# Two routed expert layers: one block for normalisation, gates and routing, a region of rows per expert, weights that are waited for expert by expert

## The reference, cut to what matters

```
def _L1_ffn_ref(inputs, gate_w, w1, w2):        # x = x + this(_layernorm(x))
    logits = tokens @ gate_w                    # (2048, 8)
    probs = softmax(logits); expert_idx = argmax(probs)
    mask1 = one_hot(expert_idx, 8)
    pos = cumsum(mask1, axis=0) - 1.0           # place of a row within its expert
    sec_mask = mask1 * one_hot(pos, 320)        # rows past 320 of an expert get nothing
    h = relu(expert_input @ w1[e])              # w1: (8, 256, 1024)
    out = probs of the expert * (h @ w2[e])     # w2: (8, 1024, 256)
def _L3_ffn_ref(x, gate_w, w1, b1, w2, b2):     # the same without a capacity,
    h = gelu(x_flat @ w1[e] + b1[e])            # with gelu and with biases
    y = h @ w2[e] + b2[e]
```

## Time and profile before

| what | value |
|---|---|
| median of 3 runs | 3418.19 us (3417.17 to 3421.18) |
| profiled execution, its own time | 3417.33 us |
| its span in the trace | 3415.7 us |
| busy: PE, DVE, ACT, POOL | 86%, 61%, 55%, 38% of the span |
| routing of layer 1 (1846.98 to 1902.96) | 55.98 us |
| routing of layer 3 (3151.09 to 3208.98) | 57.89 us |
| experts' tiles of layer 1, of layer 3 | 170.67 us, 171.63 us |

### The profile page before, as it was taken

One profiled execution on the slowest core, in us unless ns is written; L12 is line 12 of the kernel. 1 busy time (PEld: TensorE's weight loads), 2 busy tenths in 40 slices (PEclk: granted clock), 3 DMA queues, 4 the chain that ended last, 5 costly groups with the idle time before them and its releaser, 6 DMA issues. The chain is left out here.

```text
span 3415.7 us, 68343 instructions
## 1 busy us (share of the span) xinstructions
PE 2921.4 (86%) x26674; PEld 2033.7 (60%) x26675; DVE 2085.7 (61%) x3098; ACT 1895.5 (55%) x2864; POOL 1302.8 (38%) x942
## 2 busy tenths in 40 slices
PE   6779998737879998889997695979999999988596
PEld 3246665415446666456666694766666666667595
DVE  6968887587867873877873224855444444466122
ACT  3448886293558884568883111755555555456131
POOL 2259998020258883157782212720000000045212
PEclk8979999878989999989997897979999999999698
DMA  4611111200022220022214311011000000042612
GB/s 147 221 56 57 54 54 57 91 13 13 1 59 53 53 47 15 16 47 58 56 38 149 114 37 45 2 31 50 26 26 26 26 26 1 1 109 62 222 37 69
DMA packets 218052, 193.21 MB, mean 57 GB/s; under 512 B 126837, under 2 KB 176865, under 8 KB 216737
## 3 DMA queue, kind: packets, MB, share of 16 engines
q1 hardware_dynamic: 210247, 172.30, 17.4%
q0 software_dynamic: 5280, 14.42, 1.3%
q10 hardware_dynamic: 2233, 2.39, 0.2%
HBM read 112.72 MB, written 39.00 MB: 44 GB/s over the span
## 5 line engine op out<-in xcount | busy, mean ns | idle before, releaser
L2663 POOL TENSOR_TENSOR lta_p_lo<-lta_p,lta_p_hi 128x1024 f16<-128x1024 f32 x256 | 539.0, 2133 | 218.0 <-DVE lta_p_hi L2786 218.0
L2858 ACT ACTIVATE lta_p<-lta_banks,lw_gmax 128x512 f32<-128x512 f32 x512 | 324.0, 683 | 112.7 <-PE lta_banks L2701 108.4
L2769 DVE TENSOR_REDUCE lta_s_ps<-lta_s_ps 128x1 f32<-128x1101 f32 x240 | 314.1, 1309 | 106.7 <-PE lta_s_ps L2680 106.7
L3814 PE MATMUL m_y_ps<-m_w,m_hT 128*128 128x256 f16 x3072 | 355.8, 273 | 2.4 <-DVE m_hT L3972 2.4
L3802 PE MATMUL m_h_ps<-m_x,m_w 128*128 128x512 f16 x1536 | 353.1, 380 | 3.1 <-issue 3.1
L3972 DVE TENSOR_TENSOR m_hT<-m_h,m_hT 128x512 f16<-128x512 f32 x256 | 176.9, 692 | 277.0 <-ACT m_hT L3899 275.3
L3899 ACT ACTIVATE m_h<-m_h_ps,m_h_bias,m_h_scale 128x512 f32<-128x512 f32 x256 | 199.5, 779 | 261.1 <-PE m_h_ps L3802 253.0
L3814 PEld LDWEIGHTS m_y_ps<-m_w,m_hT 128*128 128x128 f16 x3072 | 299.2, 98 | 65.4 <-issue 8.2
L1242 POOL TENSOR_TENSOR c0a_tri_p_lo<-c0a_tri_p,c0a_tri_p_hi 128x1024 f16<-128x1024 f32 (+2 forms) x192 | 285.7, 1526 | 58.2 <-DVE c0a_tri_p_hi L1416 57.4
L3802 PEld LDWEIGHTS m_h_ps<-m_x,m_w 128*128 128x128 f16 x1536 | 150.5, 98 | 159.5 <-issue 5.4
L1491 ACT ACTIVATE c0a_tri_p<-c0a_banks,c_size 128x512 f32<-128x512 f32 (+3 forms) x384 | 208.4, 577 | 45.4 <-PE c0a_banks L1310 32.6
(11 more groups left out here) (760 smaller groups left out, 6582.4 us busy)
## 6 DMA issues: line engine op xcount, KB each, us to landing
m_w<-in_L_ffn_w_dram SPq DMA_DIRECT2D x4, 8192.0 KB, 40.4
m_raw<-in_L_ffn_W_dram SPq DMA_DIRECT2D x16, 1024.0 KB, 6.4
lta_q<-ltb_qT SPq DMA_DIRECT2D x96, 128.0 KB, 2.5
c_side<-in_fside_Bx16xSxS_dram SPq DMA_DIRECT2D x16, 616.0 KB, 4.7
c0a_tri_q<-c_near SPq DMA_DIRECT2D x96, 96.0 KB
c0a_tri_k<-c_mixed SPq DMA_DIRECT2D x93, 96.0 KB
lta_k<-ltb_kT SPq DMA_DIRECT2D x64, 137.6 KB, 2.6
lt_vh<-ltb_v SPq DMA_DIRECT2D x64, 128.0 KB
```

The source lines that it names most:

```text
L2663: nc.gpsimd.tensor_tensor(p_lo[:, slot, :], p32[:, p32_slot(h, j), :], p_hi[:, slot, :], ALU.subtract).then_inc(rested, 1)
L2769: nc.vector.tensor_reduce(ntop_of(h)[:, n:n + 1], scores(h, n), AX_X, ALU.max, negate=True).then_inc(top_ready, 1)
L2858: nc.scalar.activation(p32[0:rows, slot, c * 512:(c + 1) * 512], t_ps[0:rows, c, :], ACT.Exp, bias=bias, scale=p["gmax"][0:rows, 0:1]).the ...
L3814: last = nc.tensor.matmul(y_ps[:, q, 0:D], hT[:, k % 2, a, f, q * P:(q + 1) * P], w2[:, v, b, f, :], start=f == 0 and m == 0, stop=f == FC ...
```

## The change

1. **One block.** `route_tokens` no longer calls `layernorm_stage`. One block normalises, transposes, gates and routes, in groups of four tiles: `choose(g)`, `place_rows(g)` and `carry(g)` on DVE, `turn`, `gates` and `count(g)` on PE, `keep_rows` and `exponentials(g)` on ACT. The count of earlier groups is carried in `before`. DVE normalises the first eight tiles ahead, and four more after each of the first two groups is placed.
2. **A region per expert.** `sorted_x` grows to `E * T + E * P` = 17,408 rows: expert e owns the rows from e * 2048. A row's address then needs no totals, and POOL scatters group by group (`x_slot`). The compact numbering (`slot`) is kept for `sorted_y`, and a new table `row_of` says where the rows of each of the 23 tiles lie.
3. **Rows loaded by POOL.** The loads of `xs` move from SP to POOL, since their address now comes from `row_of`. For tile j POOL issues the load of tile j + 2 and then waits for `y_evac` of tile j and stores it.
4. **Weights expert by expert.** 16 transfers of 1 MB with a semaphore for each expert. In the experts' block SP waits for an expert's weights, issues a transfer of one number into `flag`, waits for it, and goes on to the next expert; `copy_w` and `reduce` wait for `expert_ready` of their expert.
5. **Zero fills.** The two stores of zeros leave the first stage. Each half of the latent attention fills one `sorted_x` (17.8 MB) with four transfers, issued by ACT after the first exponentials of heads 4, 6, 8 and 10.

```
@@ project_qkv, sync
-        for rows, kept in zip(env.sorted_x, env.zero_stored):
-            sp.dma_start(rows.rearrange("(j p) d -> p j d", p=P),
-                         env.zero[:].unsqueeze(1).to_broadcast([P, NT, D])).then_inc(kept, 16)
@@ latent_attend, scalar
+                if j == 0 and h in ZERO_AT:
+                    act.dma_start(zeros[ZERO_AT.index(h)], env.zero[:].unsqueeze(1).to_broadcast([P, SORTED_ROWS // P // ZERO_FILLS, D])
+                                  ).then_inc(env.zero_stored[b], 16)
@@ route_tokens, sync
-        sp.dma_start(w1[:], w("w1").rearrange("e (c p) f -> p e c f", p=P)).then_inc(weights_loaded, 16)
-        sp.dma_start(w2[:], w("w2").rearrange("e (c p) d -> p e c d", p=P)).then_inc(weights_loaded, 16)
+        for e in range(E):
+            sp.dma_start(w1[:, e], w("w1")[e].rearrange("(c p) f -> p c f", p=P)).then_inc(w_loaded[e], 16)
+            sp.dma_start(w2[:, e], w("w2")[e].rearrange("(c p) d -> p c d", p=P)).then_inc(w_loaded[e], 16)
@@ route_tokens, gpsimd
         for t in range(TILES):
-            nc.gpsimd.indirect_dma_start(sorted_x, bass.IndirectOffsetOnAxis(ap=slot[:, t:t + 1], axis=0),
+            if t % GROUP == 0:
+                pool.wait_ge(slot_ready, t // GROUP + 1)
+            nc.gpsimd.indirect_dma_start(sorted_x, bass.IndirectOffsetOnAxis(ap=x_slot[:, t:t + 1], axis=0),
                                          xn[:, t, :], None).then_inc(scattered, 16)
         pool.wait_ge(scattered, 16 * TILES)
@@ route_tokens, vector
+        for t in range(2 * GROUP):
+            normalise(t)
+        for g in range(groups):
+            choose(g)
+            dve.wait_ge(hot_ready, g + 1)
+            if g:
+                carry(g)
+            place_rows(g)
+            if g == 0:
+                carry(g)
+            if g + 2 < groups:
+                for t in tiles_of(g + 2):
+                    normalise(t)
@@ routed_experts, sync
-        def load(j, u):
-            if not (isinstance(j, int) and j < 2):
-                sp.wait_ge(x_turned, j - 1)
-            sp.dma_start(xs[:, u, :], sorted_x[bass.ds(j * P, P), :]).then_inc(xs_loaded[u], 16)
-        tiles(sp, load)
+        for e in range(E):
+            sp.wait_ge(w_loaded[e], 32)
+            sp.dma_start(flag[0:1, e:e + 1], env.eps[0:1, 0:1]).then_inc(expert_ready, 16)
+            sp.wait_ge(expert_ready, 16 * (e + 1))
@@ routed_experts, gpsimd
-        def store(j, u):
+        def load(j, u):
+            row = pool.value_load(row_of[0:1, bass.ds(j, 1)], min_val=0, max_val=SORTED_ROWS - P)
+            if not (isinstance(j, int) and j < 2):
+                pool.wait_ge(x_turned, j - 1)
+            nc.gpsimd.dma_start(xs[:, u, :], sorted_x[bass.ds(row, P), :]).then_inc(xs_loaded[u], 16)
+
+        def work(j, u):
+            if within(j, 2):
+                load(j + 2, u)
             pool.wait_ge(y_evac, j + 1)
             nc.gpsimd.dma_start(sorted_y[bass.ds(j * P, P), :], ys[:, u, :]).then_inc(ys_stored[u], 16)
 
-        tiles(pool, store)
+        for j in range(2):
+            load(j, j)
+        tiles(pool, work)
@@ routed_experts, tensor, reduce (and vector, copy_w)
             e = pe.value_load(expert_of[0:1, bass.ds(j, 1)], min_val=0, max_val=E - 1)
+            pe.wait_ge(expert_ready, 16 * e + 16)
```

More of the change, by code:

```diff
@@ L3055, in _ @@
     def _(pe):
[L3056 to L3059, removed]
-        nc.tensor.matmul(place_ps[:, 0:TILES * E], upto[:], hot[:].rearrange("p t e -> p (t e)"), start=True, stop=False)
-        for t in range(TILES - 1):
-            later = TILES - 1 - t
-            last = nc.tensor.matmul(place_ps[:, (t + 1) * E:TILES * E].rearrange("p (t e) -> p t e", e=E), all_ones[:],
-                                    hot[:, t:t + 1, :].to_broadcast([P, later, E]), start=False, stop=later == 1)
@@ L3065, in _, with turn, gates @@
-        last.then_inc(counted, 1)
+        def turn(t):
+            pe.wait_ge(normed, t + 1)
+            if t >= TURNED:
+                pe.wait_ge(x_evac, t - TURNED + 1)
+            for c in range(DC):
+                last = nc.tensor.transpose(x_ps[:, t % TURNED, c * P:(c + 1) * P], xn[:, t, c * P:(c + 1) * P], env.ident[:])
+            last.then_inc(x_turned, 1)
+        def gates(t):
+            g, q = divmod(t, GROUP)
+            pe.wait_ge(x_evac, t + 1)
+            if t == 0:
+                pe.wait_ge(gate_loaded, 16)
+            if q == 0 and g >= 2:
+                pe.wait_ge(shifted, g - 1)
+            for c in range(DC):
+                last = nc.tensor.matmul(lg_ps[:, g % 2, q * E:(q + 1) * E], xnT[:, c, t * P:(t + 1) * P], gate[:, c, :],
+                                        start=c == 0, stop=c == DC - 1)
+            if q == GROUP - 1:
+                last.then_inc(lg_done, 1)
@@ L3068, in _, with keep_rows, exponentials @@
             nc.tensor.transpose(b_ps[:, 0:E * FC], b1_rows[:], env.ident[0:E * FC, 0:E * FC]).then_inc(b1_turned, 1)
+        for t in range(TILES + 2):
+            if t >= 2 * GROUP and t % GROUP == 0:
+                count(t // GROUP - 2)
+            if t < TILES:
+                turn(t)
+            if t >= 2:
+                gates(t - 2)
+        count(groups - 1)
+        if b1 is not None:
+            pe.wait_ge(b1_kept, 1)
+        pe.wait_ge(carried, groups)
+        nc.tensor.matmul(b_ps[:, 0:E], all_ones[:], before[:, groups, :], start=True, stop=True).then_inc(summed, 1)
     @block.scalar
     def _(act):
-        act.wait_ge(shifted, 1)
-        nc.scalar.activation(pr[:], lg[:], ACT.Exp).then_inc(exped, 1)
+        def keep_rows(t):
+            act.wait_ge(x_turned, t + 1)
+            nc.scalar.copy(xnT[:, :, t * P:(t + 1) * P],
+                           x_ps[:, t % TURNED, 0:D].rearrange("p (c t) -> p c t", c=DC)).then_inc(x_evac, 1)
+        def exponentials(g):
+            part = slice(g * GROUP, (g + 1) * GROUP)
+            act.wait_ge(shifted, g + 1)
+            nc.scalar.activation(pr[:, part], lg[:, part], ACT.Exp).then_inc(exped, 1)
+        act.wait_ge(var_ready, 1)
+        nc.scalar.activation(rstd[:], var[:], ACT.Sqrt).then_inc(std_ready, 1)
+        nc.scalar.activation(warm[:], env.eps[:], ACT.Exp).then_inc(table_loaded, 1)
+        act.wait_ge(table_loaded, 1)
         if b1 is not None:
@@ L3076, in _ @@
             nc.scalar.copy(b1[:].rearrange("p e c -> p (e c)"), b_ps[:, 0:E * FC]).then_inc(b1_kept, 1)
-            act.wait_ge(b1_kept, 1)
+        for t in range(TILES):
+            keep_rows(t)
+            if t > GROUP and t % GROUP == 2:
+                exponentials(t // GROUP - 1)
+        exponentials(groups - 1)
     @block.vector
```

208 lines of the change are left out of this document (132 added, 76 removed).

## The result

The kernel takes 3544.31 us after the change (median of 4 runs, 3543.13 to 3547.55), against 3417.68 before (median of 4 runs). The ratio is 1.0372, with a 95% interval from 1.0354 to 1.0390: 3.7% slower. The forecast was 3485, with a range that ended at 3540. The direction was right, and about half of the loss had no term in the sum.

A forecast was written before the change was run, and what follows sets the result against it. PE bound the experts' tiles; in routing, the gates-to-scatters chain and the weight transfers ended almost together. 3415.7 + 74 - 6.6 = 3483 of span, 3485.6 with the offsets to the median, gave 3485 us; range 3440 to 3540.

The forecast's parts named there:

- Rows loaded by POOL: Experts' loop: loads behind stores land late, 1.7 us a tile in layer 1, 2.0 in layer 3; 74 us added.
- Zero fills: First stage and latent attention: removed stores and added fills count nothing; upper bound 29 us from ACT's issues.
- forecast as 8 us more: Experts' loop: a 600 ns register load on POOL would make the gap 0.9, not 0.7, adding 8 us.
- the tile's sum: Experts' loop: each of 20 tiles a layer pays the late load of rows, 34 and 40 us, 74 together.
- the 8.5 to 10 that I had named: Experts' loop, a sign to look for: tiles should take 8.5 to 10 us instead of 7.3.
- one tile in five at half speed: Experts' loop, rival: idling PE lowers the granted clock, adding 8 x 7.3 = 58 us, to 3543; chance 3%.
- Routing in groups: Routing: first scatter at 13.2 us, last from 35.4 to 39.3, end near 45, 11 us earlier than 55.98.
- Weights by expert: Start of the experts' block: first product at 55.6 and 58.5 us, gains of 3.8 and 2.8, together 6.6.
- the first rival: Experts' loop: rows arrive in time, tiles keep 7.3 us, routing's gain remains: 3411, at best 3399; chance 11%.
- The flag ahead of the queue: Start of the experts' block, bound: a flag passing SP's queued weights gives 49 and 51, gaining up to 19.
- 1.11 us for every issue: Experts' loop, upper bound: longest issues and gaps make rows 3.0 and 2.5 us late, 116 us in all.
- The sum's own range: Whole kernel: bounds of the terms added, +35 to +116 us, that is 3453 to 3534.

The follow-up runs named there:

- experiment 10: Kernel after, with POOL still waiting for tile j's results, then issuing the load of tile j + 3 ahead of tile j's store: 3509.95 us, ratio 1.0268.
- experiment 1: Kernel before, with only the loads of rows moved from SP to POOL, behind an earlier tile's store: 3543.07 us, ratio 1.0374.
- experiment 2: Kernel after, with PE reading the tile's expert and waiting for its flag ahead of the transposes instead of behind them: 3493.92 us, ratio 1.0229.
- experiment 9: Kernel after, with spare PE products in the experts' loop, 6 ahead of the transposes and 3 behind them: 3525.56 us, ratio 1.0320.
- Experiment 3: Kernel after, with POOL issuing the load of tile j + 3, not j + 2, before the store of tile j: 3412.15 us, 0.9987 of before.
- Experiment 7: Kernel after, with POOL's load one tile earlier and no flags; PE and DVE wait for all 16 weight transfers first: 3418.89 us, ratio 1.0002.
- experiment 6: Kernel before, with only the larger sorted_x and its zero fills from ACT's queue in the latent attention: 3418.33 us against 3419.59, ratio 1.0002.

## Why the prediction was right and where it failed

**Rows loaded by POOL: right in kind, and in size partly by luck.** Forecast 1.7 and 2.0 us late in 20 tiles each, 74 us; measured 1.65 and 1.75, 68 us. Inside the term two errors nearly cancelled. The gap between store and load is 0.1 us, not 0.7 or 1.2: POOL's sequencer reads the row's address (at 2031.6) while the store is still being written (2031.16 to 2032.71).

```profile
L3280 POOLq TENSOR_LOAD <-m_row_of x1: 287/287/287, 2031.6 to 2031.6; - x1
```

The stores are longer, 1.13 and 1.55 us in turn instead of 1.11 and 0.54, and the load takes 2.3 us to landing, not 2.0. A few tenths of a microsecond decide the length of a store: in layer 1 before, every second one began 0.25 us or more ahead of DVE's copy and took 0.54 us; now all but the first of these begin 0.20 to 0.23 us ahead of it and take 1.55 to 1.58. The Trainium skill, SBUF — State Buffer, section "SBUF: two separate sides", has POOL locked out of descriptor writing under such a copy; by that rule the trace agrees, in nearly every tile of layer 1 now instead of every second one. Of the Trainium skill's floor of about 600 ns for a register load (DMA: Bandwidth & Descriptors, section "Latency and other measured facts"), forecast as 8 us more: nothing of it shows where the load stands behind a store (gap 0.1 us). Where it stands alone on the path it does: experiment 10 pays 0.6 us on POOL, PE 0.76 (experiment 1). The load instruction alone took 0.29 to 0.31 us, which is under that floor; the rest is what stands around it.

**The step that failed: the tile's sum held one late load and nothing that the lateness uncovers.** It put 74 us on the loops, and they lost 125.6: 68 for the late rows, 34 for the gap behind the transposes, 23 for longer products. The tiles took 10.2 and 10.6 us in the mean, just above the 8.5 to 10 that I had named. I allowed a gap for the register load of `row_of` on POOL and said nothing of that of `expert_of` on PE, which is the same kind of instruction. It was free only because PE's sequencer ran ahead of queued products. Once it must stop at the transposes, the load behind them is paid: 34 us, of which experiment 2 gave back 32. Had I asked of every wait what stands behind it in the same queue, and what covered that until now, the sum would have been 3485 + 34 = 3519.

**The clock: a rival, right in kind and too small in chance.** I gave "one tile in five at half speed" 3%, with +58 us; 10 tiles in 40 were stretched, but for a part of one product each, 19 us in sum (experiment 9), a third of the 58. The evidence used against it, that the rows show 0.50 only where PE idles for two thirds of the time, was the wrong one: both of those stretches lie far from the case, and no row before showed a loop with PE idle for a fifth. This mechanism and the forecast don't exclude each other, and it belonged in the sum's upper side.

**Routing in groups: right.** First scatter at 13.5 us (forecast 13.2, though the three terms written for it add up to 13.0), last at 36.7 (39.3), end at 44.8 (45). The third and fourth groups ran together without a gap. The scatters landed later than I put down, 8.1 us from the start of the last one to the experts' block instead of 5.7, under the weights.

**Weights by expert: right.** First product at 54.9 and 57.3 us (forecast 55.6 and 58.5), a gain of 4.5 and 4.0 for 3.8 and 2.8. In the changed kernel nothing of it is left in the total, since 11 us went elsewhere. Experiment 3 turns the sum around: with the lateness gone, the rest of the change is worth 6.2 us by the medians and 1 to 7.5 by the interval, where 6.6 was forecast, and its time of 3412 lies at the 3411 of the first rival. Experiment 7 shows that this gain needs the flags: the shorter routing without them gives nothing. The flags without the shorter routing were not tried.

**Two bounds were added up wrong.** The flag ahead of the queue would have given 10.4 and 10.3 us, near 21 for both and not 19; and 1.11 us for every issue gives 3.0 us late for both buffers, not 3.0 and 2.5. Neither moves the forecast. The sum's own range would have reached from 3451 to some 3544, with the measured time at its end, but by too high a price of the late rows and not by the terms that were missing.

**Zero fills: right, nothing.** The issues take 0.38 us, the eight fills land after 19.4 us at the median (I had 12.4 of transfer and 2 of latency), and experiment 6 finds no difference (interval from 2 us faster to 4 slower).

## What to carry to other kernels

Before a load is moved into the queue of a store, look up which event gives its buffer back and which wait stands ahead of it in the new queue: here the buffer was free a tile earlier, and issuing the load for one tile further on was worth 132 us. When a wait becomes real on an engine that used to run ahead, what stands behind it in the same queue is uncovered too, here a register load, and the clock may follow; price the three together. And where a stage is bound by transfers, ask which of them its successor needs first: half of the weights could flow some 25 us later, beside a busy PE.

## What the runs showed of the hardware

- A register load (0.29 to 0.31 us for the instruction alone) cost at most 0.1 us in a queue that had work ahead of it: 0.1 us between store and load on POOL (none without the register load, experiment 1), and on PE 0.22 us from the transposes to the next product in the kernel before, where the load had been done 1.6 us ahead. Where the engine had just waited it cost 0.6 us on POOL and 0.76 on PE.
- A store that POOL issued beside DVE's copy into `w_mine` (1.23 us) ended 1.33 to 1.36 us after the copy's start, whether it began 0.2 us ahead of that or 0.46 behind. One that began 0.25 us or more ahead took 0.54 to 0.57 us (both kernels, experiments 1 and 3).
- The lower clock came and went with short idling: PE idle for 21% of the loops, in pieces under 2 us, gave 0.97 and 0.94; the same loops with spare products in the gaps, PE idle for 2 to 3%, gave 1.00 (experiment 9). Experiment 2, idle for 16 to 17% of its loops, had 1.00 and 0.98; experiment 10, idle for 16%, had 0.93 in both, and experiment 1, idle for 18 and 19%, 0.95 and 0.96. Why they differ is open; the profiled execution of experiment 2 took 4 us less than its median, that of experiment 10 took 12 more.
- Two fills of 17.8 MB of zeros beside the latent attention changed the time by less than 0.12% (experiment 6).
